# Two graph layers on one core: weight-block differences on GpSimd, adds between low parts, a wait per PSUM bank, x loaded ahead of the weights

## The chip, the cores and the metric

The kernel runs on one core of one Trainium2 chip. The core has TensorE (PE, with PEld for its weight loads), VectorE (DVE), ScalarE (ACT), GpSimd (POOL) and SyncE (SP, which issues the DMAs). The metric is the device time of one execution in microseconds; lower is better.

## The reference

625 nodes with 1024 features pass through two graph layers; each layer's output is added to its input and normalised over the features.

```python
# layer 0: T5 norm, relational convolution with 2 relations to 286 features, elu, product back to 1024
# layer 1:
out = x @ root + bias
for r in range(8):
    sums = segment_sum(x[src] * mask_r, dst); mean = sums / max(cnt, 1)
    out = out + mean @ weight[r]            # u
z = concatenate([u, x]) @ w_gate + b_gate
h = tanh(u) * z + x * (1 - z)
x = layernorm(x + h)
```

The work of the profile is layer 1: 8 relations with a weight of 1024x1024 each, and the x part and the u part of the gate's weight, 2048x1024 together.

## The kernel before

The nodes are padded to 640 rows, 5 tiles of 128. A gather with a sum over edges is a product with a matrix of edge counts (`cnt8`, fp16), which is built in layer 0 from one-hot columns. All fp32 products are made of fp16 parts: each operand has a high part, a rounded fp16 copy that ACT writes (for weights `step_high`, L558), and a low part, the remainder, that DVE writes (`step_low`, L1258), and three matmuls (high high, high low, low high) stand for one.

Layer 1 runs in steps. A step j takes half the columns (512) of one relation's weight, a unit; 16 steps serve the 8 relations and 2 more (16 and 17, the "gate" steps) the x part of the gate. In a step, `seven(j)` on PE multiplies x by the unit in Strassen's manner: the weight half is cut into four blocks of 128x1024 fp32 per partition, and seven products stand for eight; it has 8 parts in the order B11, T2, B21, T1, T3, T4, B12, B22, numbered 0 to 7, of 36, 24, 36, 24, 24, 24, 12 and 36 matmuls of 256 columns, each reading one block's high and low part from `wsplit` and adding into one of the five PSUM banks of `psP`. Four of the blocks (T1 to T4) are no blocks of the weight, but differences of them: first = B12 - B11, second = B22 - first, third = B21 - second (in place), fourth = B22 - B12. They are subtractions of 128x1024 fp32 from SBUF into SBUF, and DVE makes them (`first_diffs`, `third_diff`, `fourth_diff`, L1265, L1267, L1274, L1280). The differences lie in the space of `x` (the trace calls them x) and in `stage`.

While PE runs `seven(j)`, ACT and DVE prepare the unit of step j+1 in the place of the parts already used (`rel_step` on both engines), and take the banks out of PSUM: ACT copies bank 0 (L733), DVE combines banks (L1552, L1560, L1562, L1566, L1572), ACT writes the high part of the product (L730) and DVE its low part (`rest`, L1543). Both engines work through an order written out by hand; nothing is reordered. After `seven(j)`, PE runs `aggregate(j-1)`: 5 tiles of 10 matmuls of 512 columns that multiply the counts by the product of the step before, in the two banks of `psA` in turn, so that tile 2 can't start before DVE has added tile 0 to `u` (`agg_add`, L1527). DVE does all five adds as the last thing of its step, behind the low part of block 7.

GpSimd takes only the maximum of each unit over the partitions (`unit_max`, L477), from which DVE works out the scale (L1234, L1160 to L1163). ACT sums the absolute values for it, for the unit after next, at its step's end (`weight_sum`, L537). SP loads a unit as soon as its place in `stage` is free.

After step 17, u is scaled and turned (transposed) on PE by `turn(2, t, ...)` (L825) into `psA`; ACT and DVE split it (L507, L1224), ACT and DVE split the blocks of the gate's u part (L547, L1252), and ten gate products of 24 matmuls (L885) end the kernel together with DVE's normalisation. At the start SP issues the loads of the edges, x in two pieces (tiles 0 to 3; the 113 rows of tile 4) and then, without a wait, six loads of layer 0's weights.

## Time and profile before

| | us |
|---|---|
| median of 3 runs | 1048.51 (1048.09 to 1049.09) |
| the profiled execution | 1047.41 |
| its span (first to last instruction) | 1045.5 |
| layer 0, to about | 255 |
| layer 1 from the first `seven` (284.5) to the start of the last (920.1) | 636 |
| the end: last `seven`, gate products, normalisation | 125 |
| busy: PE 890.2, PE weight load 647.9, DVE 739.3, ACT 460.5, POOL 18.5 | |

PE is busy for 85% of the span and DVE for 71%. Matmuls are pipelined, so that the mean duration of one (274 ns for 256 columns) is longer than the distance from one to the next; how long a part takes is read from the starts of the parts.

### The profile page before, as it was taken

What the parts mean: (1) busy time and instruction counts of PE and PEld (TensorE: products, weight loads), DVE (VectorE), ACT (ScalarE), POOL (GpSimd) and SP (SyncE); (2) the same over time, 40 slices, a digit from 0 to 9 for tenths busy, and PEclk for the clock granted to TensorE, in tenths of its full rate; (3) what the DMA queues carried; (4) which work ended last, traced back from release to release, by engine and by line L of the source; (5) the groups of instructions that cost most, each with busy time, mean ns of one, the idle gap of its engine ahead of it and who ended that gap; (6) DMA issues with size and microseconds to landing.
All of it is one profiled execution on the core that took longest, in us unless ns stands there. A gap on an engine that the chain in (4) does not pass through costs nothing.

```text
span 1045.5 us, 18907 instructions
## 1 busy us (share of the span) xinstructions
PE 890.2 (85%) x7115; PEld 647.9 (62%) x7116; DVE 739.3 (71%) x1216; ACT 460.5 (44%) x748; POOL 18.5 (2%) x46
## 2 busy tenths in 40 slices
PE   0568998989988889889888988988988998894990
PEld 0556886744477668668667766865865776672440
DVE  3589996786996666677667667667767766744781
ACT  0683444646545453444445345244344434417200
POOL 1000001000000000000000000000000000000000
PEclk9789999999998999999999999999999999997995
DMA  4401000522022210220220221122022022101110
GB/s 150 123 3 46 1 0 5 216 106 102 1 81 82 81 58 25 82 81 0 80 80 0 80 80 30 50 80 80 0 80 80 0 81 101 62 21 59 43 61 38
DMA packets 30343, 63.43 MB, mean 61 GB/s; under 512 B 1481, under 2 KB 4689, under 8 KB 30289
## 3 DMA queue, kind: packets, MB, share of 16 engines
q1 hardware_dynamic: 30289, 62.71, 17.1%
q8 instruction: 34, 0.56, 0.2%
q14 instruction: 20, 0.16, 0.0%
HBM read 57.52 MB, written 5.18 MB: 60 GB/s over the span
## 4 chain that ended last, share of the span: by engine, by line
PE 46%; DVE 24%; issue 13%; ACT 11%; DMA 3%; DVEq 1%; ACTq 0%; SPq 0%; POOL 0%; POOLq 0%
PE psP L1034 19%; PE psA L1089 10%; DVE wsplit L1258 7%; ACT wsplit L558 7%; PE psP L836 6%; PE psP L885 4%; PE psA L874 4%; DMA x<-in_x 3%; PE psP L961 1%; DVE u_mem L1527 1%; PE psA L825 1%; DVE key_mem L1562 1%; DVE vec L1572 1%; DVE vec L1566 1%; DVE vec L1560 1%
## 5 line engine op out<-in xcount | busy, mean ns | idle before, releaser
L1034 PE MATMUL psP<-wsplit,xT 128*128 128x256 f16 x2592 | 297.2, 274 | 6.0 <-DVE p_mem L1543 5.6
L1034 PEld LDWEIGHTS psP<-wsplit,xT 128*128 128x128 f16 x2592 | 254.6, 98 | 40.6 <-DVE p_mem L1543 5.9
L1089 PE MATMUL psA<-p_mem,c_mem 128*128 128x512 f16 x800 | 178.0, 379 | 48.7 <-DVE u_mem L1527 48.7
L1089 PEld LDWEIGHTS psA<-p_mem,c_mem 128*128 (+1 forms) x800 | 77.0, 98 | 143.6 <-DVE u_mem L1527 34.9
L1034 PE MATMUL psP<-wsplit,x 128*128 128x256 f16 x1296 | 152.1, 275 | 1.7 <-DVE key_mem L1562 1.5
L1258 DVE SCALAR_TENSOR_TENSOR wsplit<-stage,sc,wsplit 128x1024 f16<-128x1024 f32 x90 | 113.9, 1283 | 37.7 <-ACT wsplit L558 37.7
L1034 PEld LDWEIGHTS psP<-wsplit,x 128*128 128x128 f16 x1296 | 127.7, 99 | 17.8 <-issue 2.2
L1527 DVE SCALAR_TENSOR_TENSOR u_mem<-psA,coef,u_mem 128x512 f32<-128x512 f32 x80 | 58.5, 748 | 73.8 <-PE psA L1089 73.8
L558 ACT ACTIVATE wsplit<-stage,sc 128x1024 f16<-128x1024 f32 x90 | 100.6, 1136 | 14.1 <-DVE sc L1163 8.1
L836 PE MATMUL psP<-p_mem 125*128 125x140 f16 x1125 | 78.6, 233 | 24.1 <-DVE p_mem L1301 17.9
L836 PEld LDWEIGHTS psP<-p_mem 125*128 125x128 f16 x1125 | 75.8, 102 | 28.3 <-issue 15.3
L558 ACT ACTIVATE wsplit<-x,sc 128x1024 f16<-128x1024 f32 x54 | 61.7, 1143 | 38.9 <-PE psP L1034 33.6
L537 ACT ACTIVATE key_mem<-stage 128x1024 f16<-128x1024 f32 x72 | 75.8, 1053 | 1.7
L1258 DVE SCALAR_TENSOR_TENSOR wsplit<-x,sc,wsplit 128x1024 f16<-128x1024 f32 x54 | 69.2, 1282 | 10.3 <-ACT wsplit L558 10.2
L1301 DVE TENSOR_SCALAR p_mem<-iota_src,key_mem 125x640 f16<-125x640 f16 x225 | 70.3, 379 | 0.0
L733 ACT ACTIVATE vec<-psP 128x512 f32<-128x512 f32 x16 | 9.5, 596 | 115.0 <-PE psP L1034 115.0
L571 ACT ACTIVATE c_mem<-psP 128x336 f32 (+1 forms) x90 | 36.8, 411 | 41.0 <-PE psP L836 41.0
L885 PE MATMUL psP<-wsplit,xT 128*128 128x512 f16 x240 | 54.0, 386 | 1.0 <-DVE u_mem L1497 1.0
L885 PE MATMUL psP<-wsplit,c_mem 128*128 128x512 f16 x240 | 52.5, 379 | 2.1 <-DVE p_mem L1673 2.1
L1298 DVE SCALAR_TENSOR_TENSOR p_mem<-iota_win,win_base,key_mem 125x560 f16<-125x560 f16 x90 | 48.2, 577 | 6.0 <-PE psP L836 2.9
L874 PE MATMUL psA<-wsplit,xT 128*128 128x429 f16 x240 | 47.0, 345 | 3.7 <-DVE wsplit L1372 2.6
L730 ACT ACTIVATE p_mem<-vec 128x512 f16<-128x512 f32 x32 | 20.2, 630 | 57.3 <-DVE vec L1566 31.3
(201 smaller groups left out, 806.1 us busy)
## 6 DMA issues: line engine op xcount, KB each, us to landing
stage<-in_L_gnn_weight SPq DMA_DIRECT2D x16, 2048.0 KB, 8.0
stage<-in_L_gnn_w_gate SPq DMA_DIRECT2D x4, 2048.0 KB, 8.0
x_home<-x SPq DMA_DIRECT2D x5, 512.0 KB, 2.6
x<-x_home SPq DMA_DIRECT2D x5, 512.0 KB, 5.6
stage<-in_L_gnn_W_rel SPq DMA_DIRECT2D x4, 572.0 KB, 11.7
x<-in_x SPq DMA_DIRECT2D x1, 2048.0 KB
xT<-in_L_gnn_root SPq DMA_DIRECT2D x1, 2048.0 KB, 8.0
stage<-in_L_gnn_root SPq DMA_DIRECT2D x1, 2048.0 KB, 8.1
```

Of the source, the lines that this page charges most:

```text
L537: nc.scalar.activation(land, st[:, part], ACT.Abs, accum_out=am[:, slot, n:n + 1]).then_inc(wsum_ready, 1)
L558: nc.scalar.activation(split_block(n, 0), step_block(REL, slot, n), ACT.Copy, scale=sc_f[:, scale_col(REL, slot), 2:3]).then_inc(whi_ready, 1)
L571: nc.scalar.activation(o8, w8, ACT.Copy)
L836: last = nc.tensor.matmul(psP[:, 2 * b + s // 3, col:col + WCOLS], src[:, s * P:(s + 1) * P], win, start=(first and s % 3 == 0), stop=Fals ...
L874: last = nc.tensor.matmul(out, lhs[:, a, c, bass.ts(t, P)], w[:, c, cols], start=first, stop=(c == chunks - 1 and a == 1))
L885: last = nc.tensor.matmul(out, lhs[:, a, c, bass.ts(t, P)], wsplit[:, s:s + 2, b, cols], start=first, stop=(c == DC - 1 and a == 1))
L1034: last = nc.tensor.matmul(psP[:, bank, (col + tt) * FB:(col + tt + 1) * FB], lhs[tt](a, c), split_block(n, b)[:, c, :], start=(first and t ...
L1089: last = nc.tensor.matmul(psA[:, (NT * h + t) % 2, :], cnt8[:, r, s, t * P:(t + 1) * P], p_part[h][a][:, s, :], start=(s == 0 and a == 0), ...
L1258: stt(split_block(n, 1), step_block(REL, slot, n), sc_f[:, scale_col(REL, slot), 2:3], split_block(n, 0), ALU.mult, ALU.subtract).then_inc ...
L1298: stt(oh_win[:, b, :, cols], w.unsqueeze(1).broadcast_to([EC, MEET, n]), wb, keyT[:, bass.ds(chunk, MEET), a:a + 1].broadcast_to([EC, MEET ...
L1301: ts(oh_src[:, b, k, :], iota_src[0:EC, :], keyT[:, chunk + k, 0:1], None, ALU.is_equal).then_inc(chunk_ready, 1)
L1527: stt(uv, psA[:, (NT * h + t) % 2, :], coef[:, t:t + 1], uv, ALU.mult, ALU.add).then_inc(agg_done, 1)
```

## The change

- The four differences of all 18 units move from DVE to GpSimd (`weight_diffs`), which does them right behind the maximum of that unit. The waits stay those of the data: the low parts of the unit before, of block 2 and of block 3.
- In `rel_step` on DVE, the low parts of blocks 5 and 6 go behind the last low part of the product, and the five adds to `u` of the step before are put between the low parts of blocks 5, 6 and 7. On ACT the high part of block 6 goes behind the last two high parts of the product.
- `seven(j)` no longer waits for all five low parts of step j-1 at its start, but for each PSUM bank ahead of the part that overwrites it.
- In the end part the same interleaving is done by hand, the turns of u's tiles 0 and 1 move into the last `seven`, behind its parts T1 and T3, and their splits move ahead of the gate's weights on both engines.
- SP waits for x before it issues layer 0's weights.

```diff
@@ sync
             st0 = unit_weights(U_W0)[0]
+            sp.wait_ge(x_loaded, 32)
             for a in range(2):
...
@@ gpsimd
-            with pool.Fori(1, UNITS // 2) as k:
+            minus = nc.gpsimd.tensor_tensor
+            def weight_diffs(j, slot):
+                pool.wait_ge(wlo_ready, weight_blocks(U_REL + j))
+                minus(t_block(0), raw_block(REL, slot, 0, 1), raw_block(REL, slot, 0, 0), ALU.subtract).then_inc(tdiff_ready, 1)
+                pool.wait_ge(tdiff_ready, 4 * j + 1)
+                minus(t_block(1), raw_block(REL, slot, 1, 1), t_block(0), ALU.subtract).then_inc(tdiff_ready, 1)
+                pool.wait_ge(tdiff_ready, 4 * j + 2)
+                pool.wait_ge(wlo_ready, weight_blocks(U_REL + j) + B21 + 1)
+                v = raw_block(REL, slot, 1, 0)
+                minus(v, v, t_block(1), ALU.subtract).then_inc(tdiff_ready, 1)
+                pool.wait_ge(wlo_ready, weight_blocks(U_REL + j) + T1 + 1)
+                minus(t_block(0), raw_block(REL, slot, 1, 1), raw_block(REL, slot, 0, 1), ALU.subtract).then_inc(tdiff_ready, 1)
...
+            unit_max(U_REL, 0)
+            pool.wait_ge(x1_kept, 16 * NT)
+            weight_diffs(0, 0)
+            unit_max(U_REL + 1, 1)
+            weight_diffs(1, 1)
+            with pool.Fori(1, SEVEN // 2) as k:
                 for s in range(2):
-                    unit_max(2 * k + s, s)
+                    unit_max(2 * k + (U_REL + s), s)
+                    weight_diffs(2 * k + s, s)
...
@@ scalar, the end part
                 nc.scalar.activation(us[:, t, :], u[:, t, :], ACT.Copy, scale=rows_f[:, 1, 2, t:t + 1]).then_inc(us_ready, 1)
+                if t == 1 or t == 3:
+                    split_hi(2, t // 2, uT, 1.0)
             raw_high(U_GU, 0)
             weight_sum(U_GU + 1, 1, slot_load(U_GU + 1))
-            split_hi(2, 0, uT, 1.0)
-            split_hi(2, 1, uT, 1.0)
@@ tensor, seven(j)
-                settled()
+                if first:
+                    pe.wait_ge(root_done, NT + 1)
+                elif gate:
+                    pe.wait_ge(zx_done, 1)
+                else:
+                    pe.wait_ge(p_lo, 5 * (j - 1) + 1)
                 blocks_ready(b0 + 1)
                 part(B11, Z, 0, x_tiles(0, 0, 1), True)
...
+                elif not gate:
+                    pe.wait_ge(p_lo, 5 * (j - 1) + 4)
                 part(B11, V, 0, x_tiles(0, 4), True).then_inc(prod, 1)
...
```

On DVE, in the step with j = 2 (the first rows of its end, from the combination of bank 2 on; L1572 combines, L1543 are low parts of the product, L1258 low parts of weight blocks, L1527 the adds to u). Before:

```order
L1258 SCALAR_TENSOR_TENSOR wsplit<-stage,sc,wsplit 128x1024 [waits whi_ready] x2
L1572 SCALAR_TENSOR_TENSOR vec<-psP,vec 128x512 [waits p16_ready,prod]
L1543 SCALAR_TENSOR_TENSOR p_mem<-psP,p_mem 128x512 [waits p_hi]
L1543 SCALAR_TENSOR_TENSOR p_mem<-vec,p_mem 128x2x256 [waits p_hi]
L1258 SCALAR_TENSOR_TENSOR wsplit<-stage,sc,wsplit 128x1024 [waits whi_ready]
L1527 SCALAR_TENSOR_TENSOR u_mem<-psA,coef,u_mem 128x512 [waits agg_full,coef_ready]
L1527 SCALAR_TENSOR_TENSOR u_mem<-psA,coef,u_mem 128x512 [waits agg_full] x4
```

The same place after (L1593 combines, L1569, L1304 and L1553 are the three others, in that order):

```order
L1593 SCALAR_TENSOR_TENSOR vec<-psP,vec 128x512 [waits p16_ready,prod]
L1569 SCALAR_TENSOR_TENSOR p_mem<-psP,p_mem 128x512 [waits p_hi]
L1569 SCALAR_TENSOR_TENSOR p_mem<-vec,p_mem 128x2x256 [waits p_hi]
L1553 SCALAR_TENSOR_TENSOR u_mem<-psA,coef,u_mem 128x512 [waits agg_full,coef_ready]
L1304 SCALAR_TENSOR_TENSOR wsplit<-stage,sc,wsplit 128x1024 [waits whi_ready]
L1553 SCALAR_TENSOR_TENSOR u_mem<-psA,coef,u_mem 128x512 [waits agg_full]
L1304 SCALAR_TENSOR_TENSOR wsplit<-stage,sc,wsplit 128x1024 [waits whi_ready]
L1553 SCALAR_TENSOR_TENSOR u_mem<-psA,coef,u_mem 128x512 [waits agg_full]
L1304 SCALAR_TENSOR_TENSOR wsplit<-stage,sc,wsplit 128x1024 [waits whi_ready]
L1553 SCALAR_TENSOR_TENSOR u_mem<-psA,coef,u_mem 128x512 [waits agg_full] x2
```

The first add stood behind the low part of block 7 and now stands right behind the last low part of the product; three low parts of weight blocks stand between the adds.

GpSimd, in one half of its loop after the change (L478 is the maximum; before, the loop held nothing else):

```order
L478 ISA ar<-am 128x4
L490 ISA
L491 ISA
L491 TENSOR_TENSOR x<-stage 128x1024
L492 ISA
L493 TENSOR_TENSOR x<-stage,x 128x1024
L494 REGISTER_ALU
L495 REGISTER_ALU
L497 TENSOR_TENSOR stage<-stage,x 128x4x256
L498 REGISTER_ALU
L499 TENSOR_TENSOR x<-stage 128x1024
```

All four differences stand in one row behind the maximum, with waits between them; on DVE they stood between the low parts.

PE at the end of the last `seven`, before (L1034 are matmuls of `seven`, L825 the turns, L885 a gate product):

```order
L1034 MATMUL psP<-wsplit,x 128x256 [waits p16_ready,wlo_ready,whi_ready]
L1034 MATMUL psP<-wsplit,x 128x256 x23
L1034 MATMUL psP<-wsplit,xT 128x256 [waits wlo_ready,whi_ready]
L1034 MATMUL psP<-wsplit,xT 128x256 x23
L1034 MATMUL psP<-wsplit,xT 128x256 [waits wlo_ready,whi_ready]
L1034 MATMUL psP<-wsplit,xT 128x256 x11
L825 MATMUL psA<-ident,c_mem 128x128 [waits turned_split,us_ready,agg_done]
L825 MATMUL psA<-ident,c_mem 128x128 x3
```

After (L1062, L851 and L911 are the same three):

```order
L851 MATMUL psA<-ident,c_mem 128x128 [waits turned_split,us_ready,agg_done]
L851 MATMUL psA<-ident,c_mem 128x128 x3
L851 MATMUL psA<-ident,c_mem 128x128 [waits turned_split]
L851 MATMUL psA<-ident,c_mem 128x128 x3
L1062 MATMUL psP<-wsplit,x 128x256 [waits p16_ready,wlo_ready,whi_ready]
L1062 MATMUL psP<-wsplit,x 128x256 x23
L851 MATMUL psA<-ident,c_mem 128x128 [waits turned_split,us_ready]
```

The first turn, which waited behind parts T4 and B12, now stands ahead of part T3, and the second behind it.

## Rows read from the trace of the kernel before

**Rows 1.** What PE waited for: operation, releaser, us in total, times, longest.
```profile
PE psA L1089 <- DVE u_mem L1527: 48.7, 16, 3.6
PE psA L825 <- DVE c_mem L1224: 13.1, 1, 13.1
PE psP L1034 <- DVE p_mem L1543: 5.6, 1, 5.6
```
**Rows 2.** Two stretches of the span: us; busy (instructions) of PE, PEld, DVE, ACT, POOL; clock; DMA.
```profile
400.00:600.00 200.00, 184.81 (x1444) 140.54 (x1442) 138.19 (x175) 86.82 (x114) 1.85 (x5) 1.00 0.15 53
600.00:940.00 340.00, 312.39 (x2410) 234.82 (x2408) 229.60 (x301) 143.50 (x190) 3.33 (x9) 1.00 0.16 57
```
**Rows 3.** Timeline of a step's end: start, us, engine, line, operation [idle before <-releaser].
```profile
499.94 6.65 PE L1089 MATMUL psA<-p_mem,c_mem 128*128 128x512 f16 x30 [3.11 <-DVE u_mem L1527]
...
506.42 4.09 PE L1034 MATMUL psP<-wsplit,xT 128*128 128x256 f16 x36
...
530.00 4.48 PE L1089 MATMUL psA<-p_mem,c_mem 128*128 128x512 f16 x20
...
532.99 0.69 DVE L1572 SCALAR_TENSOR_TENSOR vec<-psP,vec 128x512 f32<-128x512 f32 x1
...
536.61 1.40 DVE L1527 SCALAR_TENSOR_TENSOR u_mem<-psA,coef,u_mem 128x512 f32<-128x512 f32 x2
...
537.41 6.65 PE L1089 MATMUL psA<-p_mem,c_mem 128*128 128x512 f16 x30 [2.94 <-DVE u_mem L1527]
```
**Rows 4.** Groups by line: operation, count | busy us, mean ns | idle before, releaser.
```profile
L1258 DVE SCALAR_TENSOR_TENSOR wsplit<-stage,sc,wsplit 128x1024 f16<-128x1024 f32 x90 | 113.9, 1283 | 37.7 <-ACT wsplit L558 37.7
L558 ACT ACTIVATE wsplit<-stage,sc 128x1024 f16<-128x1024 f32 x90 | 100.6, 1136 | 14.1 <-DVE sc L1163 8.1 <-PE psP L1034 5.9
L1280 DVE TENSOR_TENSOR x<-stage 128x1024 f32<-128x1024 f32 x18 | 22.1, 1225 | 1.9
L730 ACT ACTIVATE p_mem<-vec 128x512 f16<-128x512 f32 x32 | 20.2, 630 | 57.3 <-DVE vec L1566 31.3 <-DVE vec L1572 26.1
```
**Rows 5.** Timeline, GpSimd alone: its largest fill, and three maxima.
```profile
0.74 0.95 POOL L445 MEMSET x<- 128x1024 f32 x1 [0.29 <-POOLq L1750]
...
159.42 3.60 POOL L477 PARTITION_ALL_REDUCE ar<-am  x1 [75.30 <-ACT stage L514]
...
256.90 1.09 POOL L477 PARTITION_ALL_REDUCE ar<-am  x1 [17.69 <-ACT p_mem L537]
...
352.42 0.37 POOL L477 PARTITION_ALL_REDUCE ar<-am  x1 [30.58 <-ACT key_mem L537]
```
**Rows 6.** Timeline, DVE beside the two long maxima.
```profile
161.22 1.57 DVE L1301 TENSOR_SCALAR p_mem<-iota_src,key_mem 125x640 f16<-125x640 f16 x5
...
256.53 1.23 DVE L1514 TENSOR_TENSOR p_mem<-p_mem,xT 128x1024 f32<-128x1024 f32 x1
```
**Rows 7.** The start, two stretches (columns as in rows 2; the last is GB/s).
```profile
12.00:15.00 3.00, 0.00 (x0) 0.00 (x0) 2.67 (x11) 0.00 (x0) 0.00 (x0) 1.00 0.06 26
...
39.00:42.00 3.00, 1.97 (x8) 1.57 (x8) 3.00 (x10) 2.57 (x6) 0.00 (x0) 0.50 0.05 17
```
**Rows 8.** The start, timeline: ACT's first work on x, DVE's wait, the first use of the weights.
```profile
30.27 1.06 ACT L495 ACTIVATE wsplit<-x 128x1024 f32<-128x1024 f32 x1 [28.25 <-DMA x<-in_x]
...
37.22 0.19 DVE L1345 RECIPROCAL rstd<-std 128x5 f32<-128x5 f32 x1 [7.13 <-ACT std L498]
...
56.42 1.00 ACT L606 ACTIVATE u_mem<-stage,lnwT 128x858 f16<-128x858 f32 x1
```
**Rows 9.** Timeline of the end part.
```profile
920.06 4.09 PE L1034 MATMUL psP<-wsplit,xT 128*128 128x256 f16 x36
...
931.41 6.23 DVE L1703 TENSOR_REDUCE rowmax<-u_mem 128x1 f32<-128x1024 f32 x5
...
953.88 1.94 PE L825 MATMUL psA<-ident,c_mem 128*128 128x128 f32 x8 [13.08 <-DVE c_mem L1224]
...
963.64 5.35 PE L885 MATMUL psP<-wsplit,c_mem 128*128 128x512 f16 x24 [2.10 <-DVE p_mem L1673]
```

99 lines of the change are left out of this document (51 added, 48 removed).

## The prediction

> **What bounds the kernel now.** I began with the list of what PE waited for, since PE is busy for 85% of the span. Its longest entry is 48.7 us in 16 waits, the matmuls of `aggregate` behind DVE's adds to u [rows 1]. Then I took the table of stretches: the clock is granted in full from 400 to 940 us and PE is busy for 92% of it [rows 2], so the loop of layer 1 is PE's work plus one regular hole. The timeline shows the hole [rows 3]. One step lasts from 499.94 to 537.41, 37.5 us. In it the three last tiles of an aggregate take 6.5 us, `seven` runs from 506.42 to 530.00 (23.6 us), two more tiles take 4.4 us, and then PE stands for 2.9 us, because tile 2 needs the bank that DVE's first add empties, and this add starts 6.6 us after `seven` has ended. Without the hole a step is 34.6 us of matmuls. Outside the loop PE loses 5.6 us once to a low part of the product, at the start of the second `seven` (no aggregate lies before it), and 13.1 us in the end part to the split of u's first turned tile [rows 1].
>
> **The adds between low parts.** I count from the end of `seven`. Today DVE goes through the last parts of the product, then waits for ACT's high part of block 7 and its own low part, and only then adds (6.6 us) [rows 3]. After the change the rows ahead of the first add are a combination and two low parts of the product, about 0.69 us each as the combination of [rows 3] shows, with ACT's two high parts of at most 0.63 us [rows 4] beside them: 2.3 us. Tile 2 needs the add at 4.4 us. The next adds can't run before their tiles are made, at 4.5, 6.7, 8.9 and 11.1 us; between two of them fit one low part of 1.28 us [rows 4] and an add of 0.7 us (two in 1.40) [rows 3]. The blocks 5 to 7 whose low parts come later than today are needed only some 25 us on. So the hole closes in every step: **-48.7 us**. The cover is 2.1 us per step (4.4 less 2.3); whatever delays DVE's first add by more opens it again. The finer waits per bank take the 5.6 us of the second `seven`, since only its third tile waits for a late low part: **-5.6 us**. In other steps the aggregate hides them and they give nothing.
>
> **The differences on GpSimd.** DVE loses four subtractions of 1.23 us in each of 18 steps [rows 4]. That is 88 us of busy time and no saving by itself, since DVE isn't the bound. The question is what they cost where they go. The trace has no two-input operation on GpSimd. Its nearest row is a fill of just such a block, one stream written, in 0.95 us [rows 5]. Two streams would be 1.9 us and three, two read and one written, one behind the other, 2.85. An estimate between these is 2.4 us, and I use both ends for the range. The trace says nothing of a second price either: what DVE and GpSimd do to each other. It has a hint. Most maxima take 0.37 us, but one took 1.09 and one 3.60 [rows 5]. The first ended 0.23 us after a DVE subtraction with two inputs in SBUF that had started before it, the other 0.23 us after a run of DVE operations on SBUF [rows 6]. DVE was not slower in either. I take it that a GpSimd operation and a DVE operation with two SBUF inputs exclude each other, whichever starts second waiting. The low parts of weight blocks are such operations.
>
> The Trainium skill, in "SBUF — State Buffer", section "Who interferes with whom", states this rule: a DVE instruction with two SBUF inputs contends with a GpSimd instruction that reads SBUF, and the second to issue blocks until the first is done. The two long maxima agree for GpSimd as the loser; no row here shows DVE as the loser. Its "GPSIMD Engine Reference", section 3.1, gives 4497 ns for a two-input add of 2048 fp32, which makes an estimate of 2.3 us for 1024, and advises against such work on GpSimd; no row here shows that price.
>
> The first and second difference of a unit run in the aggregate, well ahead of use. The third and fourth are on a chain. With g for one difference and exclusion, counted from the start of a `seven`: block 2's low part ends at 13.6 us; the third difference ends at 13.8+g; block 3's low part (1.28) follows, then the fourth difference ends at 15.3+2g; ACT's high part (1.14) and the low part (1.28) of block 4, two combinations, a high part, and the remaining low parts of the product end with the first add at 22.6+2g. Tile 2 needs that at 28.1, so the hole stays shut up to g = 2.7. With 2.4 the loop is PE's. Behind the fourth difference on GpSimd waits the maximum of the next unit; it is wanted 9 us after the end of `seven`, the fourth ends 3 us before it, so 12 us cover it. The waits per bank on PE name combinations that are over before an aggregate's 11 us are. In the first steps there is less room, as no aggregate lies between the first two `seven` and DVE starts the unit late. Worked through in the same manner with g = 2.4, PE waits 1.6 us for ACT's copy of bank 0, 1.3 for the combination of bank 2, 3.6 for a low part in the second `seven`, 3.0 for the copy again, and 2.9 for the first add: 12.4, of which 1.5 is there today: **+11 us**, with exclusion. Without it the same walk gives 3; with g = 1.9 and exclusion also 3; with g = 2.85 and exclusion 21, since then the hole of the loop is open by 0.3 us a step too.
>
> **The end part.** Today 43.6 us pass from the start of the last `seven` to the first gate product (920.06 to 963.64), [rows 9], of which PE waits 13.1 us for the split of the first turned tile [rows 1]: ACT has its part of the split behind all of the gate's weights. New, from that start: the last add ends at 1.0, the scales of the gate, five row maxima at 1.25 each [rows 9], an evacuation between them and the row scales end at 9.8, u's scaled tiles are there at 10.9 and 12, the first turn runs at 13.1 behind part T1, its split is out of the way by 16, the second turn runs at 16.9, ACT's four high parts of the gate's weights end at 24.4 and DVE's low parts at about 27. The first gate product starts at 27.4: **-16.2 us**. The third gate product then waits 1.7 us for the low parts of the other half: **+1.7 us**. The ten products and DVE's end follow as today.
>
> **x ahead of the weights.** From 12 to 15 us, with the first piece of x in and no weights moving, the DMA moves 26 GB/s at 6% of 16 engines [rows 7]: this is one engine at work, on the second piece of x (452 KB, 17 us at this rate). x is complete at 30.27 and DVE waits 7.13 us behind it [rows 8]. Without the weights in between it ends about 2 us sooner: **-2 us**. The weights now start at 28 instead of 4; their 3.5 MB need some 13 us, and their first use is at 56 [rows 8]. That cover of some 15 us hides them, and also the two bias loads that stand behind them on SP; gone, it would cost what is over.
>
> **The sum.** 1045.5 - 48.7 - 5.6 + 11 - 16.2 + 1.7 - 2 = 985.7 us of span. Outside it lie 1.9 us of the profiled execution (1047.41), which is 1.1 us below the median, so 988.7; rounded, **988 us**.
>
> **The rivals.**
> - *No exclusion* (17%). The maxima were long for another reason. The early steps cost 3 in place of 11: 980 us. For it: DVE was never slowed; against: both long maxima ended with DVE's work.
> - *GpSimd sets the step, still faster* (15%). With g from 2.9 to 4.0, or with GpSimd held off by DVE's run of low parts as in the 3.60 us maximum, a step is 34.6 + 2(g - 2.7) us: 35.6 at 3.2 and 37.2 at 4.0. Over 14 steps, and with the early steps at 15 to 20, that gives 1007 to 1040.
> - *Slower* (7%): the same chain with g above 4.2. A step is then over 37.6, the hole is wider than today's, and from about 4.4 on the rest of the change (some 10 us net) is used up as well; at g = 5 the loop alone loses 25 us net and the kernel takes about 1075. Against it: this is more than four fills' time for one block; for it: a 3.60 us wait has been seen, and four differences stand in each step.
> - *The change doesn't do what it says* (5%): the hole closes, but the clock of PE doesn't hold once PE never stops. From 39 to 42 us it is granted at half [rows 7], so it isn't a constant; 3% less over the 560 us of the loop is 17 us, 1005. Against it: full clock at 92% busy [rows 2].
>
> **How the numbers follow.** The forecast has 54%: 979 to 998 by g from 1.9 to 2.85. With *no exclusion* (978 to 984) it makes 71%. To leave out no more than two in ten the range takes the lower part of the third rival and the clock: **976 to 1008**. About 0.2% is what a measurement of this kernel can tell from no change. Faster by more than that 91%, the same 2%, slower 7%.
>
> **What the profile after would show.** A step of 34.6 to 34.7 us and no entry of `aggregate` behind the adds of more than some 5 us, or the chain is wrong. The first add 2.3 to 4 us after `seven`'s end. A GpSimd difference of 1.9 to 2.85 us (its spans are rough; the distance from one semaphore to the next decides). With exclusion, low parts of 1.28 us that are stretched or start late beside a difference; without, all at 1.28. The first gate product 27 us after the last `seven` began. ACT's first work on x at 28. Wrong would make it: a difference over 2.9 us, a wait of PE for blocks (`wlo_ready`) inside a `seven` of the loop, or a granted clock below 1.00 from 400 us on.

## The result

| | before | after |
|---|---|---|
| median of 4, us | 1048.8 (1048.09 to 1049.31) | 1160.13 (1159.6 to 1160.65) |
| the profiled execution, us | 1047.41 | 1160.56 |
| its span, us | 1045.5 | 1158.5 |
| mean granted clock of PE | 0.965 | 0.911 |
| layer 1, from the start of the first `seven` to the start of the last, us | 635.6 | 765.8 |
| the end, from the start of the last `seven`, us | 125.4 | 109.0 |

The ratio is 1.106, with a 95% interval from 1.104 to 1.108: the change makes the kernel 10.6% slower, where 988 us had been forecast. The end part gained what it was to gain, and more. The steps of layer 1 lost 130 us. One execution, of the run with a fill below (1000.81 us at a mean granted clock of 0.921, where its three others took 979 to 980 at 0.967 to 0.969), belongs to a slower state of the chip and is left out.

What PE waited for, after (columns as in [rows 1]; L1062 is `seven`, L1132 `aggregate`; L1553 are the adds to u, and L1585 is the combination that part B22 waits for, `c22_ready`):

```profile
PE psP L1062 <- DVE key_mem L1585: 121.6, 16, 8.9
...
PE psA L1132 <- DVE u_mem L1553: 7.2, 10, 1.1
```

The hole of 48.7 us behind the adds [rows 1] is nearly closed, as forecast. In its place PE waits 7.6 us in each of 16 steps inside `seven`, ahead of B22, for a combination on DVE. The table of stretches has the same in other words, against [rows 2]: PE is busy for 82% of these stretches and not 92%, DVE for 46% and not 68%, and the granted clock is no longer 1.00.

```profile
400.00:600.00 200.00, 164.12 (x1149) 117.21 (x1150) 96.72 (x134) 76.91 (x105) 50.68 (x22) 0.89 0.12 42
600.00:940.00 340.00, 278.45 (x2045) 206.35 (x2043) 151.21 (x216) 120.71 (x160) 83.76 (x39) 0.91 0.14 49
```

All engines but GpSimd are less busy than before, so the loop has become a chain with gaps. One step of it, in the timeline of the kernel after (columns as in [rows 3]); it answers to the step in [rows 3] and lasts from 555.58 to 600.39, 44.8 us:

```profile
553.97 0.19 ACT L563 ACTIVATION_READ_ACCUMULATOR key_mem<-stage 128x1 f32 x1
...
563.60 0.39 POOL L478 PARTITION_ALL_REDUCE ar<-am  x1 [21.91 <-issue]
564.02 0.16 DVE L1280 TENSOR_REDUCE asum<-ar 128x1 f32<-128x4 f32 x1 [7.22 <-POOL ar L478]
...
564.84 1.15 ACT L584 ACTIVATE wsplit<-stage,sc 128x1024 f16<-128x1024 f32 x1 [4.53 <-DVE sc L1209]
...
571.36 2.34 POOL L491 TENSOR_TENSOR x<-stage 128x1024 f32<-128x1024 f32 x1 [7.37 <-issue]
573.78 2.34 POOL L493 TENSOR_TENSOR x<-stage,x 128x1024 f32<-128x1024 f32 x1
576.16 1.15 ACT L584 ACTIVATE wsplit<-x,sc 128x1024 f16<-128x1024 f32 x1 [10.17 <-POOL x L493]
...
577.34 1.28 DVE L1304 SCALAR_TENSOR_TENSOR wsplit<-x,sc,wsplit 128x1024 f16<-128x1024 f32 x1 [9.43 <-ACT wsplit L584]
...
580.49 3.33 POOL L497 TENSOR_TENSOR stage<-stage,x 128x1024 f32<-128x1024 f32 x1 [4.37 <-DVE wsplit L1304]
...
582.25 0.69 DVE L1585 SCALAR_TENSOR_TENSOR key_mem<-psP,vec 128x512 f32<-128x512 f32 x1
...
583.08 4.70 PE L1062 MATMUL psP<-wsplit,x 128*128 128x256 f16 x24 [7.68 <-DVE key_mem L1585]
583.63 0.74 DVE L1569 SCALAR_TENSOR_TENSOR p_mem<-key_mem,p_mem 128x512 f16<-128x512 f32 x1 [0.70 <-ACT p_mem L756]
583.78 2.79 POOL L499 TENSOR_TENSOR x<-stage 128x1024 f32<-128x1024 f32 x1
...
587.62 1.47 PE L1062 MATMUL psP<-wsplit,xT 128*128 128x256 f16 x12
...
593.10 0.74 DVE L1553 SCALAR_TENSOR_TENSOR u_mem<-psA,coef,u_mem 128x512 f32<-128x512 f32 x1
...
593.90 6.65 PE L1132 MATMUL psA<-p_mem,c_mem 128*128 128x512 f16 x30 [0.49 <-DVE u_mem L1553]
```

Follow it by its rows. ACT's last weight sum is over at 554.16, and GpSimd has done nothing since the last difference of the unit before; still the maximum starts 9.4 us later, at 563.60. It is over at 563.99, everything that the first difference waits for was there at 553.9, and it starts 7.4 us later, at 571.36. Both gaps are "issue": the engine waited for nothing that the profile shows. (The 21.91 us in the row of the maximum are the whole idle time ahead of it; 12.5 of them lie before the weight sum was over.) The difference itself is as quick as had been estimated, 2.34 us. But ACT has the high part of T2 (block 1) next in its order and stands for 10.2 us behind the second difference, DVE stands for 9.4 behind ACT, and the combination for B22 stands on DVE behind that. So PE gets it 7.7 us late. It then runs B22 at half clock for a while (24 matmuls in 4.5 us and not 2.6), which adds 1.9 us. These two and the 0.5 us ahead of `aggregate` are 10.1 of the 10.4 us by which this step (44.8) is longer than a step of PE's work alone (34.4, below).

The lines of GpSimd in the page's part of groups say that this is every step (18 units; columns as in [rows 4]):

```profile
L478 POOL PARTITION_ALL_REDUCE ar<-am x23 | 13.8, 598 | 571.0 <-issue 375.4
...
L497 POOL TENSOR_TENSOR stage<-stage,x 128x1024 f32<-128x1024 f32 x18 | 58.8, 3269 | 85.2 <-DVE wsplit L1304 85.2
...
L491 POOL TENSOR_TENSOR x<-stage 128x1024 f32<-128x1024 f32 x18 | 42.8, 2380 | 130.0 <-issue 130.0
```

130.0 us in 18 gaps is 7.2 us ahead of each first difference.

```
L478 ISA [waits wsum_ready]
L478 ISA ar<-am 128x4
L490 ISA
L491 ISA
L491 TENSOR_TENSOR x<-stage 128x1024 [waits wlo_ready]
```

The wait for the weight sums stands ahead of the exchange, so it can't start ahead of its time, although the last difference was over 12 us earlier. The theory: the two exchanges are the whole loss. Its rivals: A, the differences cost it, being slow or held off by DVE; B, the new order of the adds or the waits per bank stall PE.

### The profile page after: what moved, and what is told of

Its sections match the earlier page's. It is cut to its first block, busy times and chain, and to the rows that moved or that the text cites. A ratio compares the mean times of both kernels' runs of the same rounds, so it can differ in the third digit from the quotient of the medians.

```text
span 1158.5 us, 18979 instructions
## 1 busy us (share of the span) xinstructions
PE 929.2 (80%) x7115; PEld 663.8 (57%) x7116; DVE 652.1 (56%) x1144; ACT 458.1 (40%) x748; POOL 213.0 (18%) x118
## 4 chain that ended last, share of the span: by engine, by line
issue 35%; PE 20%; DVE 14%; ACT 13%; POOL 13%; DMA 2%; DVEq 1%; ACTq 0%; POOLq 0%; SPq 0%
ACT wsplit L584 8%; PE psP L862 5%; PE psP L911 4%; PE psA L900 4%; POOL x L499 4%; DVE wsplit L1304 4%; POOL x L493 3%; POOL x L491 3%; PE psP L1062 3%; ACT key_mem L563 3%; DMA x<-in_x 2%; POOL stage L497 2%; PE psP L987 1%; DVE wsplit L1298 1%; PE psA L1132 1%
## 5 line engine op out<-in xcount | busy, mean ns | idle before, releaser
L1062 PE MATMUL psP<-wsplit,xT 128*128 128x256 f16 x2592 | 298.1, 274 | 5.4 <-ACT vec L759 2.9
L1062 PE MATMUL psP<-wsplit,x 128*128 128x256 f16 x1296 | 186.9, 312 | 134.5 <-DVE key_mem L1585 121.6
L1062 PEld LDWEIGHTS psP<-wsplit,xT 128*128 128x128 f16 x2592 | 255.4, 99 | 41.6 <-issue 3.2
L1062 PEld LDWEIGHTS psP<-wsplit,x 128*128 128x128 f16 x1296 | 142.4, 111 | 172.0 <-issue 139.5
L1304 DVE SCALAR_TENSOR_TENSOR wsplit<-x,sc,wsplit 128x1024 f16<-128x1024 f32 x54 | 71.0, 1314 | 216.5 <-ACT wsplit L584 216.5
L1132 PE MATMUL psA<-p_mem,c_mem 128*128 128x512 f16 x800 | 177.1, 379 | 7.2 <-DVE u_mem L1553 7.2
L1132 PEld LDWEIGHTS psA<-p_mem,c_mem 128*128 (+1 forms) x800 | 77.3, 98 | 100.9 <-DVE u_mem L1553 8.3
L1304 DVE SCALAR_TENSOR_TENSOR wsplit<-stage,sc,wsplit 128x1024 f16<-128x1024 f32 x90 | 114.6, 1277 | 21.1 <-ACT wsplit L584 21.1
L478 POOL PARTITION_ALL_REDUCE ar<-am x23 | 13.8, 598 | 571.0 <-issue 375.4
L497 POOL TENSOR_TENSOR stage<-stage,x 128x1024 f32<-128x1024 f32 x18 | 58.8, 3269 | 85.2 <-DVE wsplit L1304 85.2
L1280 DVE TENSOR_REDUCE asum<-ar 128x1 f32<-128x4 f32 x22 | 3.4, 156 | 123.9 <-POOL ar L478 123.9
L1553 DVE SCALAR_TENSOR_TENSOR u_mem<-psA,coef,u_mem 128x512 f32<-128x512 f32 x80 | 59.7, 746 | 20.6 <-PE psA L1132 20.6
L491 POOL TENSOR_TENSOR x<-stage 128x1024 f32<-128x1024 f32 x18 | 42.8, 2380 | 130.0 <-issue 130.0
L911 PE MATMUL psP<-wsplit,xT 128*128 128x512 f16 x240 | 54.3, 387 | 1.0 <-DVE u_mem L1522 1.0
L911 PE MATMUL psP<-wsplit,c_mem 128*128 128x512 f16 x240 | 52.5, 379 | 1.7 <-DVE wsplit L1298 1.7
```

What stands on the lines that cost most here:

```text
L491: minus(t_block(0), raw_block(REL, slot, 0, 1), raw_block(REL, slot, 0, 0), ALU.subtract).then_inc(tdiff_ready, 1)
L497: minus(v, v, t_block(1), ALU.subtract).then_inc(tdiff_ready, 1)
L911: last = nc.tensor.matmul(out, lhs[:, a, c, bass.ts(t, P)], wsplit[:, s:s + 2, b, cols], start=first, stop=(c == DC - 1 and a == 1))
L1062: last = nc.tensor.matmul(psP[:, bank, (col + tt) * FB:(col + tt + 1) * FB], lhs[tt](a, c), split_block(n, b)[:, c, :], start=(first and t ...
L1132: last = nc.tensor.matmul(psA[:, (NT * h + t) % 2, :], cnt8[:, r, s, t * P:(t + 1) * P], p_part[h][a][:, s, :], start=(s == 0 and a == 0), ...
L1304: stt(split_block(n, 1), step_block(REL, slot, n), sc_f[:, scale_col(REL, slot), 2:3], split_block(n, 0), ALU.mult, ALU.subtract).then_inc ...
```

## Experiments on the cause

### The differences back on DVE

The kernel after with one part undone (three more such lines each for the first unit and for the gate):

```diff
@@ gpsimd: weight_diffs is gone
@@ vector, rel_step
                 unit_scale(j + (U_REL + 1), 1 - slot, REL)
+                first_diffs(j + 1, 1 - slot)
...
                 step_low(j + 1, 1 - slot, 2)
+                third_diff(j + 1, 1 - slot)
                 step_low(j + 1, 1 - slot, 3)
+                fourth_diff(j + 1, 1 - slot)
```

> The changed kernel with one part undone: the four differences of each unit are back on DVE, at the places that they had before; GpSimd takes the maxima only. Adds between low parts, waits per bank, end part and x ahead of the weights stay. Theory (GpSimd's code for tensor_tensor and for the all-reduce is exchanged twice a unit, 7 us behind the maximum and 9.4 us ahead of the next one): no exchange is left in the loop, the step is PE's work, 34.7 us, and the kernel takes about 982 us, ratio 0.937 to before. Rival A (the differences themselves are the cost, slow on GpSimd or held off by DVE): the same 982. Rival B (the new order of the adds or the waits per bank stall PE): the differences don't matter, and it stays within 1130 to 1160.

Measured: 975.59 us, ratio 0.930 (0.928 to 0.931), 6 us less than expected. Rival B is out: all its parts are in this kernel. The differences or what comes with them cost 184.5 us. The stretches:

```profile
400.00:600.00 200.00, 200.00 (x1541) 150.51 (x1540) 150.06 (x194) 96.04 (x129) 2.41 (x6) 1.00 0.18 63
600.00:860.00 260.00, 260.00 (x2014) 196.88 (x2013) 196.22 (x250) 126.77 (x168) 2.85 (x7) 1.00 0.17 59
```

PE is never idle from 400 to 860 us, at full clock, and a step takes 34.4 us. DVE, with the differences, is busy for 75%: it had the room.

### Only the differences moved

The kernel before, and from the change this alone:

```diff
@@ gpsimd, the loop; weight_diffs as in the change
-                    unit_max(2 * k + s, s)
+                    unit_max(2 * k + (U_REL + s), s)
+                    weight_diffs(2 * k + s, s)
@@ vector, rel_step
-                first_diffs(j + 1, 1 - slot)
...
-                third_diff(j + 1, 1 - slot)
...
-                fourth_diff(j + 1, 1 - slot)
```

> The kernel before with one part of the change alone: the four differences go to GpSimd behind the maximum of their unit; everything else is as before. Theory (code exchange): the two exchanges delay the scale and block T2 as in the changed kernel, and the adds at the step's end come later still: a step of about 47 us in place of 37.5, 1200 to 1235 us, ratio 1.15 to 1.18, slower than the whole change. Rival A: the cost of the differences alone, the same direction; with only their 10.9 us of busy time a step, 1040 to 1060. Rival B (order of adds, waits per bank): 1035 to 1050, since neither is in it.

Measured: 1186.75 us, ratio 1.131 (1.129 to 1.133); the direction is the theory's, the size below its range. Alone, the move costs 138 us. PE's waits show where: at the same combination (here L1563), and at the adds, which stand at the end of a DVE order that now runs late.

```profile
PE psA L1114 <- DVE u_mem L1531: 108.6, 16, 12.4
...
PE psP L1059 <- DVE key_mem L1563: 34.6, 16, 9.1
```

### A fill in place of the maximum

This separates the exchange from the differences. The kernel after, with the maximum over the partitions left out:

```diff
@@ gpsimd, unit_max
-                nc.gpsimd.partition_all_reduce(ar[:, slot, 0:parts], am[:, slot, 0:parts], P, RMAX).then_inc(max_ready, 1)
+                if parts == 4:
+                    nc.gpsimd.memset(ar[:, slot, 0:parts], 27.0).then_inc(max_ready, 1)
+                else:
+                    nc.gpsimd.partition_all_reduce(ar[:, slot, 0:parts], am[:, slot, 0:parts], P, RMAX).then_inc(max_ready, 1)
```

> The changed kernel with the maximum over the partitions left out for all units from the root weights on: at its place, with the same waits and the same semaphore, GpSimd fills the four values with 27.0, which gives every unit but those of the gate the power of two that the maximum would have given (the gate's scale is then one power off). A fill stands between the differences, and they are no different. Theory (code exchange): fills and subtractions follow each other without an exchange, the gaps of 7 and 9.4 us vanish, a step is 34.7 us and the kernel takes 985 to 991 us, ratio about 0.94; this is the case that the prediction worked out. Rival A (slow differences, or DVE and GpSimd excluding each other): the differences are all there, so it stays at 1140 to 1160. Rival B: also 1140 to 1160.

(Of the gate's units it says too much: their sum, 77, lies between the same powers of two as the other units' 108, so the constant gives every unit its own scale.)

Measured: 979.75 us (979.17 to 980.40), ratio 0.934 (0.932 to 0.936), 5 us under the expected range. All four differences are on GpSimd, and the kernel is only 4.2 us slower than with them on DVE: rival A is out, but for these 4.2, which all lie in the way from the first `seven` to the third (69.4 us, 65.2 with the differences on DVE). Timeline of GpSimd around one start of a unit, and ACT's high part of block 1, which is made of the second difference; the gaps are gone:

```profile
591.58 0.10 POOL L479 MEMSET ar<- 128x4 f32 x1 [12.62 <-ACT key_mem L566]
591.71 2.36 POOL L494 TENSOR_TENSOR x<-stage 128x1024 f32<-128x1024 f32 x1
...
594.15 2.35 POOL L496 TENSOR_TENSOR x<-stage,x 128x1024 f32<-128x1024 f32 x1
...
600.60 1.15 ACT L587 ACTIVATE wsplit<-x,sc 128x1024 f16<-128x1024 f32 x1 [1.08 <-PE psP L1065]
```

The fill starts 0.14 us behind the last weight sum, the first difference behind the fill at once. In the order of this kernel no exchange stands between the two. The second difference is over at 596.50, and ACT takes it 4.1 us later, released by PE. The fill takes away the all-reduce itself too, 0.4 us a unit; the next experiment keeps it.

### An exchange with no work to it

The reverse: differences on DVE, and GpSimd gets a subtraction that costs nothing.

```diff
@@ gpsimd, the differences on DVE
                     unit_max(2 * k + (U_REL + s), s)
+                    pool.wait_ge(spare_done, (2 * k + s) * 1)
+                    nc.gpsimd.tensor_tensor(spare[:, 2, :], spare[:, 0, :], spare[:, 1, :], ALU.subtract).then_inc(spare_done, 1)
```

In a second kernel the wait is for twice the count, and behind the subtraction stands

```diff
+                    nc.gpsimd.partition_all_reduce(spare[:, 3, 0:1], spare[:, 0, 0:1], P, RMAX).then_inc(spare_done, 1)
```

> The changed kernel with the differences back on DVE, and on GpSimd behind each maximum one subtraction of 128x8 on a spare tile, for which nobody waits. It keeps the exchange of code and takes the differences' work away. Theory (code exchange): the exchange behind the maximum is in nobody's way, but the one back to the all-reduce can only start when the weight sums are there and delays the maximum, and with it the scale and block 0, by some 9.4 us in each unit. A step of 36.5 us in place of 34.4, about 1015 us, ratio 0.96 to 0.975, that is 40 us slower than with no exchange (975.6). Rival A (the differences' own time is the whole cost): a subtraction of 8 columns costs nothing, 976 us.

> As the run with the subtraction of 128x8, and behind it an all-reduce of one column on the spare tile, for which nobody waits either. Theory (code exchange): both exchanges (about 11 us beside the load of the weights and 6 us without one) now run in the 34 us in which GpSimd has nothing to do, the maximum finds its code in place, and the time is that of the kernel with the differences on DVE, 975 to 978 us, with as many exchanges as before. If an exchange costs something beyond its place (DMA or DVE disturbed), it is over 980.

Measured: 1007.29 us for the first (0.960 to 0.963 of before), 974.62 us for the second (0.929 to 0.931). Eight columns cost 32 us (40 were expected); the same with an all-reduce more, which brings the code back early, costs nothing. The number of exchanges is the same in both, two a unit. What counts is whether one has to run between a result and the instruction that waits for it. The eighteen all-reduces more in the second cost nothing either. The two timelines of GpSimd (first run, then second); in the first the weight sums are over at 567.40, in the second at 585.65:

```profile
540.85 0.39 POOL L481 PARTITION_ALL_REDUCE ar<-am  x1 [28.18 <-issue]
548.42 0.88 POOL L500 TENSOR_TENSOR spare<-spare 128x8 f32<-128x8 f32 x1 [7.18 <-issue]
576.84 0.39 POOL L481 PARTITION_ALL_REDUCE ar<-am  x1 [27.54 <-issue]
```

```profile
551.60 0.38 POOL L481 PARTITION_ALL_REDUCE ar<-am  x1 [17.93 <-ACT key_mem L555]
563.21 0.20 POOL L502 TENSOR_TENSOR spare<-spare 128x8 f32<-128x8 f32 x1 [11.23 <-issue]
569.42 0.82 POOL L503 PARTITION_ALL_REDUCE spare<-spare  x1 [6.01 <-issue]
585.86 0.43 POOL L481 PARTITION_ALL_REDUCE ar<-am  x1 [15.61 <-ACT key_mem L555]
```

In the first the maximum starts 9.4 us behind the weight sums, in the second 0.2. The second row of the second run, an exchange of 11.2 us that nobody waits for, is the longest seen.

### One of the two exchanges hidden in the changed kernel

```diff
@@ gpsimd, weight_diffs, its last lines
                 minus(t_block(0), raw_block(REL, slot, 1, 1), raw_block(REL, slot, 0, 1), ALU.subtract).then_inc(tdiff_ready, 1)
+                nc.gpsimd.partition_all_reduce(spare[:, 0:1], spare[:, 1:2], P, RMAX)
```

> The changed kernel with one instruction more per unit: behind the fourth difference GpSimd does an all-reduce of one column on a spare tile, which nobody waits for. Theory (code exchange): the exchange towards the all-reduce then runs in GpSimd's idle time, 16 us before the weight sums are ready, and the maximum starts 0.2 us behind the last weight sum and not 9.4; the exchange of 7 us behind the maximum stays. The step falls from 45.3 to about 36.2 us and the kernel takes 1015 to 1030 us, ratio 0.97 to 0.98. Rival A and Rival B: an instruction more changes nothing or costs 0.4 us a unit, 1160 to 1168.

Measured: 1064.13 us, ratio 1.014 (1.011 to 1.016). The exchange ahead of the maximum is hidden and 96 us come back, as the theory has it and its rivals don't, but not the 130 to 145 that were expected: a step takes 39.2 us (565.94 to 605.17) and not 36.2. The timeline of GpSimd tells why:

```profile
558.01 0.38 POOL L502 PARTITION_ALL_REDUCE spare<-spare  x1 [5.93 <-issue]
564.84 0.38 POOL L480 PARTITION_ALL_REDUCE ar<-am  x1 [6.45 <-ACT key_mem L566]
576.07 2.34 POOL L493 TENSOR_TENSOR x<-stage 128x1024 f32<-128x1024 f32 x1 [10.85 <-issue]
```

The exchange ahead of the first difference takes 10.85 us here, and took 7.4 in the changed kernel. What differs is what the DMA does meanwhile. The load of the next unit (2 MB) is issued as a step ends. From 565 to 570 us in this run the DMA engines are busy for 92% and move 303 GB/s; during the exchange at 552 to 558 they move nothing:

```profile
552.00:558.00 6.00, 6.00 (x37) 3.60 (x36) 3.78 (x5) 3.93 (x6) 0.08 (x1) 0.96 0.00 0
...
565.00:570.00 5.00, 5.00 (x44) 4.03 (x42) 1.56 (x7) 0.00 (x0) 0.22 (x1) 1.00 0.92 303
```

In the changed kernel it is the exchange ahead of the maximum that has the load beside it (9.4 us), and the next one that has not:

```profile
555.00:563.00 8.00, 8.00 (x72) 6.88 (x71) 0.98 (x2) 0.60 (x1) 0.00 (x0) 1.00 0.77 262
563.00:571.00 8.00, 8.00 (x76) 7.17 (x74) 2.57 (x7) 1.15 (x1) 0.39 (x1) 1.00 0.00 0
```

Over all loops from 330 us on in the runs with exchanges, the one towards the all-reduce takes 5.7 to 6.3 us with the DMA still and the one towards the subtraction 6.7 to 7.8; beside a load of weights, or a part of one, they take 7.3 to 11.2. In the rows above each is some 3.5 us longer beside the load (9.4 against 5.9, 10.85 against 7.4). That the code comes by DMA and has to share it is the obvious reading; no run took the load away to show it. The expected number had been worked out with one duration for all.

## Experiments on the other parts

### The adds between low parts, alone

The kernel before, with this from the change (on ACT the high part of block 6 moves as well):

```diff
@@ vector, rel_step
                 rest(3, high_rows, left, p1_tmp)
-                step_low(j + 1, 1 - slot, 5)
-                step_low(j + 1, 1 - slot, 6)
...
                 rest(5, low_rows, right, p16_tmp)
+                if agg:
+                    agg_add(agg[0], 1 - slot, 0)
+                step_low(j + 1, 1 - slot, 5)
+                if agg:
+                    agg_add(agg[0], 1 - slot, 1)
+                step_low(j + 1, 1 - slot, 6)
+                if agg:
+                    agg_add(agg[0], 1 - slot, 2)
                 step_low(j + 1, 1 - slot, 7)
                 if agg:
-                    agg_add(agg[0], 1 - slot)
+                    agg_add(agg[0], 1 - slot, 3, 4)
```

> The kernel before with one part alone: the adds to u between the low parts of blocks 5 to 7, and the high part of block 6 later on ACT. The prediction gave -48.7 us for it, all of PE's hole behind the adds. 998 to 1002 us, ratio 0.953. The wait of PE for the adds falls from 48.7 us to under 5, a step from 37.5 to 34.4. Rival: the low parts of blocks 5 to 7 now come later and the hole opens elsewhere in the step, 1015 or more.

Measured: 998.17 us, ratio 0.953 (0.951 to 0.954): 50.6 us, where the prediction had 48.7. A step takes 34.4 us (521.65 to 556.02). PE's wait for the adds is one of 3.6 us, in the last step, whose adds this kernel leaves where they were. The 5.6 us at the start of the second `seven` [rows 1] fall to 3.0 by the adds alone:

```profile
PE psA L1089 <- DVE u_mem L1528: 3.6, 1, 3.6
PE psP L1034 <- DVE p_mem L1544: 3.0, 1, 3.0
```

### A wait per bank, and x ahead of the weights, each alone

Two kernels, each the kernel before with one of these edits:

```diff
@@ tensor, seven(j)
-                settled()
+                elif gate:
+                    pe.wait_ge(zx_done, 1)
+                else:
+                    pe.wait_ge(p_lo, 5 * (j - 1) + 1)
...
+                elif not gate:
+                    pe.wait_ge(p_lo, 5 * (j - 1) + 4)
...
+                    pe.wait_ge(p167_ready, j)
...
+                    pe.wait_ge(c12_ready, j)
...
+                    pe.wait_ge(c21_ready, j)
```

```diff
@@ sync
             st0 = unit_weights(U_W0)[0]
+            sp.wait_ge(x_loaded, 32)
```

> The kernel before with one part alone: PE waits for each PSUM bank ahead of the part that overwrites it. The prediction gave -5.6 us, the wait for the low parts of the product at the start of the second seven. In the order of the kernel before no other step has such a wait, since the aggregate lies between. 1043 to 1045 us, ratio about 0.995. Rival (the finer waits stall PE in every step): 16 steps of some 0.3 us or more, over 1050.

> The kernel before with one part alone: SP waits for x before it issues layer 0's weights. The prediction gave -2 us, from a DMA engine that is free of the weights' share sooner. ACT's first work on x was 1.45 us earlier in the changed kernel's trace (28.82 against 30.27), so 0 to -2 us: 1046.5 to 1048.5, ratio 0.998 to 1.000. Rival: the weights come too late and something of layer 0 waits for them, over 1049.

Measured: 1054.23 us for the waits (12 executions from 1046.9 to 1056.6; ratio 1.0043, 1.002 to 1.0066) and 1046.26 us for x (ratio 0.9995, 0.997 to 1.0015). By these intervals neither gives a gain that can be told from none, and the waits look 0.4% slower when alone. For x there is more to see in the single executions: ten of its twelve took 1045.1 to 1047.6 us and two 1055.4 and 1055.9, and of the kernel before, beside it, 22 of 23 took 1047.2 to 1049.8 and one 1057.4. The medians are 2.1 us apart, as forecast; the few long executions widen the interval over it, so a gain of 2 us is likely and not settled. In the profiled execution of the waits (1047.17 us) the 5.6 us of [rows 1] are gone; smaller waits stand in their place, in the same second `seven`:

```profile
316.43 6.35 PE L1034 MATMUL psP<-wsplit,xT 128*128 128x256 f16 x36 [5.65 <-DVE p_mem L1543]
```

is the row of before, and

```profile
317.31 1.48 PE L1036 MATMUL psP<-wsplit,xT 128*128 128x256 f16 x12 [2.24 <-DVE p_mem L1558]
...
323.57 6.71 PE L1036 MATMUL psP<-wsplit,xT 128*128 128x256 f16 x60 [2.15 <-ACT vec L733]
```

are those with the waits per bank; the hole behind the first adds grew from 2.9 to 3.6 us too. From the first `seven` to the third, 2.5 us are left of the 5.6. Why nine of its twelve executions took 1052 to 1057 us can't be said; the profile is of one of the three others, and the nine had a mean granted clock of 0.955 to 0.960 in place of 0.962 to 0.965. So what the waits do alone stays open.

Whether the waits are worth anything once the adds are in their new place, two kernels told, side by side: the one with the differences back on DVE, and the same with one wait again:

```diff
@@ tensor, seven(j)
                 else:
-                    pe.wait_ge(p_lo, 5 * (j - 1) + 1)
+                    pe.wait_ge(p_lo, 5 * j)
...
-                elif not gate:
-                    pe.wait_ge(p_lo, 5 * (j - 1) + 4)
...
-                    pe.wait_ge(p167_ready, j)
...
-                    pe.wait_ge(c12_ready, j)
...
-                    pe.wait_ge(c21_ready, j)
```

> The changed kernel with two parts undone: the differences are on DVE, and PE waits at the start of a seven for all five low parts of the step before, as in the kernel before. It tells what the waits per bank are worth in the kernel in which PE is never idle from 400 to 860 us. In the trace with the adds alone PE waited 3.0 us there, once, in the second seven, and with the waits per bank 2.8 us for another thing at the same place; so 0 to +3 us against the waits per bank (974 to 978 us where that run is again 975.6). Rival (the prediction's 5.6 us): 981.

> The changed kernel with the differences back on DVE, once more and with more executions, beside the same kernel with one wait for all low parts. Expected 974 to 977 us, ratio 0.928 to 0.931.

Measured: 974.86 us with one wait, 974.35 with a wait per bank, each at 0.929 (0.927 to 0.932). The waits per bank are worth nothing here that can be measured.

### All but the end part

The kernel before with the three edits of this chapter together, so that against the first experiment only the end part is as before.

> The kernel before with three parts of the change: adds between low parts, a wait per bank, x ahead of the weights; the end part and the differences (on DVE) are as before. Against it the run with the differences on DVE (975.6 us) has the end part more, which the prediction gave 14.5 us and the changed kernel's trace, from the start of the last seven to the end, 16.4 (125.4 before, 109.0 after). So 990 to 992 us, ratio 0.945. Rival: the end part's gain is only there because the step ahead of it was late; then this is nearer to 976.

Measured: 996.30 us, ratio 0.951 (0.949 to 0.953), 4 us over the expected range. Against the 975.59 us with the end part as changed, that part is worth 20.7 us. In the traces it is 15.4 us from the start of the last `seven` on (124.5 to 109.1), and 4.6 us ahead of it: the step before the last `seven` is 5.5 us longer, where the old order still has its hole of 3.6 us and the 30 matmuls behind the hole take 8.34 us and not 6.65. The expected number had left that step out. The turn that PE waited 13.1 us for [rows 9] is there in this run as before, and not in the kernel after, where it stands inside `seven`:

```profile
903.14 1.94 PE L826 MATMUL psA<-ident,c_mem 128*128 128x128 f32 x8 [13.08 <-DVE c_mem L1240]
```

```profile
1062.64 1.04 PE L851 MATMUL psA<-ident,c_mem 128*128 128x128 f32 x8
...
1076.71 5.34 PE L911 MATMUL psP<-wsplit,c_mem 128*128 128x512 f16 x24 [1.68 <-DVE wsplit L1298]
```

### The account

| step from kernel to kernel | us |
|---|---|
| before, to the adds alone | -50.6 |
| to waits per bank and x first as well | -1.9 |
| to the end part as well (differences on DVE) | -20.7 |
| to the differences on GpSimd, without an exchange (fill for maximum) | +4.2 |
| to the changed kernel: the exchanges, with what they bring (the half clock behind each wait, the all-reduce's own 0.4 us) | +180.4 |
| sum | +111.4 |

The best version is the change without its first line: differences on DVE, 974 to 976 us, 7% faster than before.

## Why the prediction was wrong

**The step that failed** is the price of a difference on GpSimd. The prediction took its busy time, 2.4 us, for the whole price, asked what DVE and GpSimd do to each other in SBUF, and came to "With 2.4 the loop is PE's". It put the passage from the all-reduce to the subtractions and back at nothing, without a reason. The runs show it at 7.2 us behind each maximum and 9.6, in the mean, ahead of the next, both between a result and what waits for it: 180.4 us in the kernel, a step of 44.8 us and not 34.6. Three statements rest on it. "The first and second difference of a unit run in the aggregate, well ahead of use": they stand behind the maximum, and the maximum waits for the last weight sum, which is over as the aggregate ends. At their own price the second is over only 4.1 us ahead of its use (run with the fill); with 9.4 us ahead of the maximum and 7.4 behind it they set the chain to block 1, and ACT waits 10.2 us. "Behind the fourth difference waits the maximum of the next unit; ... 12 us cover it": the fourth difference was long over, but the exchange waits with the maximum for the weight sums, and no idle time ahead of them covers it. And the rival *Slower* was tied to a difference of more than 4.2 us. It came out slower with a difference of 2.34.

**What could have been read.** Two rows at the start of the kernel before, in the timeline of GpSimd, hold the price:

```profile
9.26 0.28 POOL L448 TENSOR_SCALAR_AFFINE_SELECT ident<-ident 128x128 f32<-128x128 f32 x1 [7.43 <-issue]
...
19.57 0.63 POOL L471 PARTITION_ALL_REDUCE u_mem<-u_mem  x1 [7.84 <-issue]
```

**Right, with their sizes.** The chains in which no exchange stands came out nearly as worked out; the run with the fill is near the kernel that the prediction described, and it took 979.75 us where 988 were forecast (its sum, 988.7, would round to 989). Of the rivals' sums, the 1075 us at g = 5 don't come out of the terms given (1048.5 + 25 - 10 is 1063), nor quite the 1040 at g = 4.0 (988 + 36 + 9 is 1033); nothing rests on either.
- *g = 2.4.* An undisturbed difference takes 2.34 to 2.36 us. As the middle between two guesses from a fill, that it came so close is in part luck.
- *The hole behind the adds, -48.7.* -50.6 alone, of which some 2.6 are from the second `seven`. A step of PE's work is 34.4 us, forecast 34.6.
- *Exclusion, from the two long maxima* [rows 5, 6]. It is there, and DVE can be the loser. In the run with the fill the third difference starts ahead of a low part, and the low part, 1.28 us as a rule, takes 2.58; in the changed kernel the low part is first, and the third difference takes 3.33 us and not 2.34 (the row at 580.49 above).

```profile
573.10 2.35 POOL L500 TENSOR_TENSOR stage<-stage,x 128x1024 f32<-128x1024 f32 x1 [10.88 <-DVE wsplit L1307]
573.95 2.58 DVE L1307 SCALAR_TENSOR_TENSOR wsplit<-x,sc,wsplit 128x1024 f16<-128x1024 f32 x1 [0.93 <-ACT wsplit L587]
```

That the second one waits until the first is done is also what the Trainium skill says in "SBUF — State Buffer", "Who interferes with whom"; these two rows bear it out in both directions. Here the second grows by a little less than what was left of the first: by 1.3 us of 1.5, and by 1.0 of 1.1. Whether exclusion also made the two long maxima long, no run tells.
- *The early steps, +11.* Too much: in the run with the fill the way from the first `seven` to the third takes 69.4 us, and 65.2 with the differences on DVE and 71.7 before. The walk with exclusion would give 74.2 (71.7 - 2.9 - 5.6 + 11), that without 66.2. So exclusion costs, but 3 us over the walk without it and not 8.
- *The end part, -14.5.* -16.4 from the start of the last `seven` (125.4 to 109.0) in the changed kernel. The first gate product starts 27.2 us behind it (1049.54 to 1076.71), forecast 27.4. What did not come is the wait of 1.7 us ahead of the third product: the row of L911 above is followed by the turn of another tile and then by 72 matmuls without a gap from 1082.76 on.

**Right in the mechanism, worth less.** *The waits per bank, -5.6:* the wait of 5.6 us for the late low part becomes one of 2.2, and the next part of the same `seven` waits for ACT's copy of bank 0 and then longer for DVE's first add; 2.5 us are left in the trace and none in the time. *x first, -2:* ACT's first work on x starts at 28.82 (28 forecast, 30.27 before), 1.45 us earlier; the medians are 2.1 us apart, inside an interval that includes zero.

**The clock rival** was about a PE that never stops. With PE at 100% from 400 to 860 us it was granted in full. It was the other way round: in the changed kernel, behind each of the 16 waits of 6.3 to 8.9 us, B22 began at half clock (its 24 matmuls have rows of 4.1 to 5.3 us there, and of 2.8 elsewhere). Of the signs of being wrong that the prediction names, two came, neither for the reason given: the clock, and a difference over 2.9 us (the third, 3.27 in the mean, behind a low part). The wait inside `seven` was for a combination and not for blocks.

## To carry to other kernels

Before work goes to GpSimd, look at which of its instructions already stand on both sides: an all-reduce and a subtraction of two tensors in turns bring an exchange at each passage, at 6 to 11 us, and a fill does not. In the profile it is an "issue" gap ahead of the first instruction of the other kind, and one such gap early in the program is enough to price it. If the turns can't be avoided, put an instruction of the coming kind, that waits for nothing, into the engine's idle time: the exchange waits with the instruction behind it, and does not start ahead by itself.

## What the runs showed of the hardware

- Passing between `partition_all_reduce` and `tensor_tensor` on GpSimd costs time in which the profile shows no instruction. With the DMA still it is 5.7 to 6.3 us towards the all-reduce and 6.7 to 7.8 towards the subtraction; beside a load of 2 MB, or a part of it, 7.3 to 11.2 us. A `memset` on either side costs none.
- GpSimd's subtraction of 128x1024 fp32 from SBUF into SBUF takes 2.34 us, DVE's 1.23 [rows 4]. A low part on DVE and such a subtraction don't run side by side; whichever starts second gets longer by nearly the rest of the first (2.58 in place of 1.28, 3.33 in place of 2.34).
- After 7.7 us without a matmul PE was at half clock (granted 0.50 from 583 to 586 us): 24 matmuls of 256 columns took 4.5 us in place of 2.6.
